# Local attention with queries transposed ahead of all scores; causal attention transposing 64-row halves in pairs; last attention mending its diagonal in 64-row halves

## The reference

```python
q = q * cos * scale + rotate_half(q) * sin * scale     # k likewise
sim = jnp.einsum('bhwie,bhwje->bhwij', bq, bk2) * QK_SCALE   # own window and the one before
attn = jax.nn.softmax(jnp.where(mask, -max, sim), -1)
out = jnp.einsum('bhwij,bhwje->bhwie', attn, bv2)
```

```python
sim = einsum('bhid,bhjd->bhij', q, k) - abs(i - j) * slope[h];  sim = where(causal, -max, sim)
out = einsum('bhij,bhjd->bhid', softmax(sim), v) @ w_out + b_out
```

```python
logits = einsum('bhqd,bhkd->bhqk', q, k) / SCALE - softplus(decay_alpha)[h] * abs(q - k)
out = einsum('bhqk,bhkd->bhqd', softmax(logits), v) @ out_w.T + out_b
```

## Time and profile before

| | |
|---|---|
| time, median of 3 runs | 4435.03 us (4434.4 to 4439.9) |
| profiled execution, its own time | 4430.25 us |
| span in its profile | 4428.5 us, mean granted TensorE clock 0.926 |
| busy | PE 3915.2 us (88%), DVE 3103.5 (70%), ACT 2556.6 (58%), POOL 1247.7 (28%) |

### The profile page before, as it was taken

How to read it: one execution, slowest core, us unless ns; L and a number is a source line. 1 busy time by engine, 2 the same in 40 slices (tenths; PEclk the granted TensorE clock), 3 DMA queues, 4 the chain that set the end, 5 groups by cost and what they waited for, 6 DMA issues and landing times.

```text
span 4428.5 us, 113349 instructions
## 1 busy us (share of the span) xinstructions
PE 3915.2 (88%) x46366; PEld 2158.4 (49%) x46462; DVE 3103.5 (70%) x5185; ACT 2556.6 (58%) x3768; POOL 1247.7 (28%) x1082
## 2 busy tenths in 40 slices
PE   3789999999999999867778999999997599999997
PEld 1365555555555555535553555555553233333333
DVE  7788888888888888645414666666664677777772
ACT  5456666666666667552224555555553276767774
POOL 0366656655566566310000000000000011111220
PEclk7899999999999999965578999999998699999998
DMA  0222222222222222201000000000000300000000
GB/s 18 71 67 75 69 65 80 71 72 74 65 76 72 68 76 68 55 10 24 21 9 17 3 4 4 4 2 4 4 1 26 100 19 20 19 20 19 19 2 15
DMA packets 85355, 166.74 MB, mean 38 GB/s; under 512 B 23336, under 2 KB 37336, under 8 KB 83568
## 3 DMA queue, kind: packets, MB, share of 16 engines
q1 hardware_dynamic: 84816, 159.13, 13.8%
HBM read 40.60 MB, written 8.52 MB: 11 GB/s over the span
## 4 chain that ended last, share of the span: by engine, by line
PE 46%; issue 19%; POOL 15%; DVE 12%; ACT 5%; DMA 1%; SPq 1%; POOLq 0%; DVEq 0%; ACTq 0%
POOL arena L987 7%; POOL arena L991 6%; PE banks L1287 6%; PE banks L2237 5%; PE banks L1270 4%; PE banks L1258 4%; ACT arena L2373 2%; PE banks L522 2%; PE banks L2195 2%; PE banks L2211 2%; PE banks L1306 1%; DVE arena L861 1%; DVE arena L1438 1%; PE banks L2215 1%; PE banks L605 1%
## 5 line engine op out<-in xcount | busy, mean ns | idle before, releaser
L2447 DVE TENSOR_REDUCE arena<-banks 128x2 f32<-128x1024 f32 x512 | 614.2, 1223 | 248.6 <-PE banks L2202 140.4
L2373 ACT ACTIVATE arena<-banks 128x1024 f32<-128x1024 f32 x512 | 522.8, 1025 | 252.7 <-PE banks L2218 134.2
L987 POOL TENSOR_TENSOR arena<-arena 128x512 f32<-128x512 f32 x384 | 424.5, 1127 | 637.4 <-DVE arena L870 629.8
L991 POOL TENSOR_TENSOR arena<-arena 128x1024 f32<-128x1024 f32 x192 | 533.1, 2776 | 15.1
L1438 DVE CUSTOM_DVE_ANT_0 arena<-arena,banks 128x512 f32<-128x512 f32 (+3 forms) x640 | 361.9, 603 | 202.6 <-issue 201.3
L1381 ACT ACTIVATE arena<-banks 128x512 f32<-128x512 f32 (+3 forms) x320 | 170.2, 532 | 401.7 <-PE banks L1270 401.0
L522 PE MATMUL banks<-arena 128*128 128x512 f32 x768 | 366.7, 622 | 30.8 <-issue 15.0
L2237 PE MATMUL banks<-arena 128*32 128x256 f32 x4096 | 334.4, 393 | 14.2 <-issue 8.7
L1518 POOL COPY arena<-arena 128x512 f32<-128x512 f32 x32 | 19.6, 613 | 1123.5 <-DVE arena L1464 1123.5
L1373 ACT ACTIVATE arena<-arena 128x128 f32<-128x128 f32 (+15 forms) x256 | 328.6, 1285 | 11.3 <-DVE arena L1450 6.3
L1258 PE MATMUL banks<-arena 64*128 64x512 f32 (+3 forms) x1280 | 322.3, 581 | 5.1 <-issue 3.8
(11 more groups left out here) (433 smaller groups left out, 7384.3 us busy)
## 6 DMA issues: line engine op xcount, KB each, us to landing
arena<-arena SPq DMA_DIRECT2D x768, 64.0 KB
arena<-arena SPq DMA_DIRECT2D x96, 384.0 KB, 3.6
arena<-arena SPq DMA_DIRECT2D x96, 128.0 KB, 3.4
arena<-in_lf_wqkv SPq DMA_DIRECT2D x6, 1024.0 KB, 6.0
arena<-features_k SPq DMA_DIRECT2D x32, 128.0 KB
arena<-arena SPq DMA_DIRECT2D x8, 512.0 KB
arena<-features_q SPq DMA_DIRECT2D x16, 216.0 KB
arena<-in_lf_wqkv SPq DMA_DIRECT2D x6, 512.0 KB, 3.8
```

The source lines that it names most:

```text
L987: nc.gpsimd.tensor_tensor(r[:, :, e * H2:(e + 1) * H2], q[:, j, :, (1 - e) * H2:(2 - e) * H2], s[:, j, 1, e * H2:(e + 1) * H2].unsqueeze(1 ...
L991: nc.gpsimd.tensor_tensor(a, a, lf_rb, ALU.add).then_inc(S("lf_rot" + x), 1)
L2373: nc.scalar.activation(bi_PT[n % 4], PS[:, 2 * bi_slot("S", n):2 * bi_slot("S", n) + 2].rearrange("p a b -> p (a b)"), ACT.Exp).then_inc(S ...
L2447: nc.vector.tensor_reduce(bi_max[j % 2][:, t, :, c], PS[:, 2 * slot:2 * slot + 2], AX.X, ALU.max).then_inc(S("bi_mx"), 1)
```

## The change

It has three parts.

1. Local attention: `scores` is one piece again instead of two halves, and `turn_q(s-1)` stands ahead of it, right behind `qk(s)`.
2. Causal attention: each 128 x 128 transpose becomes two, of the block's lower and upper 64 rows, 64 moving columns each. The lower halves of both heads go to bank 4, the upper ones to bank 5, and `at_PT` has one buffer for both heads. A turn starts only when both copies of the last one are done, and it signals both copies at its end. A `sem_inc` on TensorE carries the waits (one in each turn, two where b is 0). The copies have as many elements as before, in runs of 64.
3. Last attention: each mending is twelve matmuls of 64 rows, heads alternating, instead of six of 128; the two halves of the triangle are separate operands (`bi_trib` doubles, `bi_tri` triples to 384 KB and holds 64-row identities too), and the slopes are copied once for each half of the partitions (two short VectorE copies at the start).

```diff
@@ lf_pe, step
                 if lf_live(s, end):
                     qk(s, l)
-                if lf_live(s - 2, end):
-                    scores(s - 2, l, end, 0)
                 if lf_live(s - 1, end):
                     turn_q(s - 1, l, end)
                 if lf_live(s - 2, end):
-                    scores(s - 2, l, end, 1)
+                    scores(s - 2, l, end)
@@ at_pe, turn
+                n = min(4, at_row(c, x) + 1 - 4 * b)
+                if i >= 1:
+                    pe.wait_ge(S("at_ptA"), l * 80 + i)
+                    pe.wait_ge(S("at_ptB"), l * 80 + i)
                 for h in range(2):
                     if b == 0:
                         pe.wait_ge(S("at_exp"), l * 64 + (2 * (2 * c + x) + h + 1))
-                    if i >= 1:
-                        pe.wait_ge(S("at_ptB" if h else "at_ptA"), l * 80 + i)
-                    for j in range(min(4, at_row(c, x) + 1 - 4 * b)):
-                        m = nc.tensor.transpose(PS[:, 4 + h, j * P:(j + 1) * P], ck(at_E[c % 2][x][h], 4 * b + j, P), ident)
-                    m.then_inc(S("at_trB" if h else "at_trA"), 1)
+                        pe.sem_inc(S("at_turning"), 1)
+                    elif h == 0:
+                        pe.sem_inc(S("at_turning"), 1)
+                    for j in range(n):
+                        k = h * n + j
+                        lower = nc.tensor.transpose(PS[:, 4, k * at_D:(k + 1) * at_D], ck(at_E[c % 2][x][h], 4 * b + j, P)[0:at_D], ident[0:at_D, 0:at_D])
+                        upper = nc.tensor.transpose(PS[:, 5, k * at_D:(k + 1) * at_D], ck(at_E[c % 2][x][h], 4 * b + j, P)[at_D:P], ident[at_D:P, at_D:P])
+                lower.then_inc(S("at_trA"), 1)
+                upper.then_inc(S("at_trB"), 1)
@@ at_dve, turned (at_act's is the same for bank 5, columns at_D to P)
-                nc.vector.tensor_copy(at_PT[x][0][:, 4 * b:4 * b + n, t % 2 * P:(t % 2 + 1) * P],
-                                      PS[:, 4, 0:n * P].rearrange("p (a b) -> p a b", b=P)).then_inc(S("at_ptA"), 1)
+                nc.vector.tensor_copy(at_PT[x][:, :, 4 * b:4 * b + n, t % 2 * P:t % 2 * P + at_D],
+                                      PS[:, 4, 0:n * P].rearrange("p (h a b) -> p h a b", h=2, b=at_D)).then_inc(S("at_ptA"), 1)
@@ bi_pe, scores (logits likewise, with bi_trib's first half)
-                    for h in range(2):
-                        for x in range(3):
-                            m = nc.tensor.matmul(PS[:, 2 * slot + h, n:n + P], ck(bi_aI[p], 2 * x + h, P), bi_trib[:, P:2 * P], start=False, stop=x == 2)
+                    for y in range(6):
+                        for h in range(2):
+                            m = nc.tensor.matmul(PS[:, 2 * slot + h, n:n + P], ck(bi_aI[p], y, P)[rows(h)], ck(bi_trib, 2 + y % 2, P)[rows(h)], start=False, stop=y == 5)
```

More of the change, by code:

```diff
@@ L1166, in program @@
         at_E = [[[arena.f32(n) for _ in range(2)] for n in (T // 2, T)] for _ in range(2)]
-        at_PT = [[arena.f32_3(n, 2 * P) for _ in range(2)] for n in (NB // 2, NB)]
+        at_PT = [arena.f32(2 * n * 2 * P).rearrange("p (h k q) -> p h k q", h=2, k=n) for n in (NB // 2, NB)]
         at_mx = [arena.f32_3(2, 4) for _ in range(2)]
@@ L2033, in program @@
         bi_cut = arena.bf16(bi_H)
-        bi_slope = arena.f32_3(8, 8)
-        bi_a = [arena.f32(8) for _ in range(2)]
-        bi_tri = arena.f32(2 * P)
-        bi_trib = arena.bf16(2 * P)
+        bi_slope = arena.f32_3(8, 11)
+        bi_a = [arena.f32(11) for _ in range(2)]
+        bi_tri = arena.f32(6 * P)
+        bi_trib = arena.bf16(4 * P)
         bi_aI = [arena.bf16(6 * P) for _ in range(2)]
@@ L2492, in slopes @@
                 pool.wait_ge(S("bi_sa"), n + 1)
[L2493 to L2494 removed]
+                for y in range(6):
+                    m = nc.gpsimd.tensor_tensor(ck(bi_aI[p], y, P), ck(bi_tri, 4 + y % 2, P), bi_a[p][:, 8 + y // 2:9 + y // 2].broadcast_to([P, P]), ALU.mult)
                 m.then_inc(S("bi_ai"), 1)
```

51 lines of the change are left out of this document (26 added, 25 removed).

## The result

| | before | changed kernel |
|---|---|---|
| median | 4434.72 us (4 runs, 4429.8 to 4439.9) | 4356.83 us (4 runs, 4354.12 to 4366.32) |
| ratio to before | | 0.9828, 95% interval 0.9809 to 0.9847 |
| profiled execution, its span | 4428.5 us | 4352.3 us |

A forecast was written before the change was run, and what follows sets the result against it. TensorE was taken to bound causal and last attention, the order of waits the local one; 80 + 31 - 1.5 + 12 = 121.5 us off 4430.25 gave 4309, 4313 from the median, with 8 in 10 inside 4270 to 4378.

The forecast's parts named there:

- the first rival: Causal attention: a 64-row transpose's load takes 0.109 us, so only switches are saved there; 4373 us, chance 13%.
- The transposes' stream, 102 us: Causal attention: a pair of half transposes takes 0.062 us instead of 0.109 per block, over 2176 blocks, 102 us of TensorE.
- the slower rival: Causal transposes: the two halves' loads go one after the other, 0.109 each, a pair 0.218; 4609 us, chance 6%.
- the 129 us: Causal attention: TensorE time saved in all, by the transposes' stream and the net gain from switches.
- The causal switches, net 27: Causal attention: scores and turns share a shape, saving 37 and 12 us; 128-row work behind turns costs 22.
- What comes late next, 48 us: Causal attention: around short turns VectorE allows little of TensorE's saving; 1.5 us lost in each of 32 pairs of steps.
- The clock: Granted clock: the prediction read it as 2.4 GHz in causal and last attention and had no term for a fall.
- Increments, 0: Causal attention: TensorE's 448 `sem_inc`s taken as free; rival that they drain TensorE, 4398 us, chance 4%.
- The rival of the full gain: Causal and last attention: later long units absorb VectorE's lag and the held-back time comes too; 4274 us, chance 9%.
- the 11 us: Last attention, logits units: the part of 21 us saved there that is given back as waiting for VectorE.
- Last attention, 31 less 1.5: Last attention: mendings lose 42 us of switches, 21 + 10 counted; larger `bi_tri` and copies at the start cost 1.5.
- Local attention, 12 us: Local attention: switches between scores and transposes go, 0.21 us in 61 waits of L876, less 1 us for GpSimd's rotation.

The follow-up runs named there:

- e11_deep: Changed kernel with a turn's lower halves of both heads all before the upper ones, and mendings in alternating runs of three: 4403.62 us, ratio 0.9930.
- e8_late: Changed kernel with 192 more increments in causal turns, and local queries' transposes ahead of the mask only in three steps of four: 4352.71 us, ratio 0.9805.
- e1_a: Kernel before with only the local attention's part of the change: 4435.24 us, ratio 0.9996.
- e4_bc: Changed kernel with the local attention's part undone, so the causal and last attention's parts only: 4356.82 us, ratio 0.9818.
- e9: Changed kernel, causal attention: output projection ahead of the turn in an odd step's first unit, VectorE's normalisation ahead of logits: 4360.14 us, ratio 0.9835.
- e10: e9 plus, in an odd step's third unit, the first projection piece ahead of the turn and VectorE's L1481 ahead of logits: 4336.44 us, ratio 0.9777.
- e5_serial: Changed kernel with all lower, then all upper halves in each head's piece of a turn, and mendings six per head in a row: 4380.18 us, ratio 0.9869.
- e3_c: Kernel before with only the last attention's part of the change: 4398.25 us, ratio 0.9918.
- e12_act_copy_first: e10 plus ScalarE's copy of the turn ahead of its long exponential in a step's first two units: 4359.07 us, ratio 0.9823.
- e2_b: Kernel before with only the causal attention's part of the change: 4400.21 us, ratio 0.9922.
- e6_copy_first: Changed kernel with the local attention as before and VectorE's copy of a turn ahead of the next logits in all causal units: 4416.74 us, ratio 0.9952.
- e7_copy_first_some: Changed kernel with the local attention as before and VectorE's copy ahead of the logits in two causal units of ten: 4399.55 us, ratio 0.9915.

## Why the prediction was right, and where it was not

- **Direction, size, range**: faster, by 78 instead of 122 us, inside the range, outside the forecast's own range of 4285 to 4345. The causal attention missed by 40 us and the local one by its whole 12, against 11 us too little in the last. That the time is inside the range is in part luck: the part of the range above 4345 was there for the first rival (4373), whose mechanism is refuted, and another cost filled it.
- **The transposes' stream, 102 us**: right. The pair goes at 0.062 us, and the loads of one half follow each other at 0.06. My sign for the slower rival, halves over 0.03 us apart, was a bad one: 97 of 219 full turns show it and still keep the step of 0.062. The first rival, a load of 0.109, is refuted, and with it, for these loads, the rule of the Trainium skill ("TensorE: Matmul & The Clock Gate", "LDWEIGHTS (loading the stationary operand)") that it came from. The slower rival, halves one after the other, is refuted as well, but e11_deep shows that it lay near: with eight of a half in a row the causal part gives nothing. The stream is four fifths of the 129 us, not five sixths.
- **The causal switches, net 27**: some 15. By the distances between starts TensorE saves about 118 us, not 129. Scores to turn gains 0.09 and not 0.15 (the last score to the first transpose 0.52, now 0.43). Turn to 128-row work costs 0.09, not 0.15, but a projection piece of two matmuls now takes 1.06 us to the scores behind it instead of 0.95, and the output projection nearly as much more, 11 us in 114 places, which the sum has at nothing. Why is open.
- **What comes late next, 48 us**: the term that was sized too small. The place was right, the price was not: I let the stretch of the earlier trace rows shrink by 0.4 us, and it did not shrink at all (8.12 and 8.12); of its three likes one shrank by 0.25 us and two grew, by 0.08 and 0.68. I had looked for the limit in VectorE, 0.7 us of room, and between its copies 0.3 us did come. What took it back is what I had named last, ScalarE's long exponentials ahead of a copy that the next turn wants for both heads. I also had one wait per pair of steps, and the trace shows two to four, of 0.2 to 1.0 us. The waits came to about 69 us, from 118 less 40 less 9 for the clock; those that the profile names grew by 56.
- **The clock**: not in the prediction at all. In the changed kernel it fell in three places and at the branch's end, some 9 us, and in no kernel without the 64-row transposes.
- **Increments, 0**: right (e8_late).
- **The rival of the full gain** was added up wrong: the 48 and the 11 us are 59, not 40, so it stands for 4254 us and not 4274, outside the range that was to hold most of it.
- **Last attention, 31 less 1.5**: mechanism right, the give-back too high. The switches that go are worth 42 us, and 40.5 came: of the 11 us that I held back for VectorE in the logits units, 5 show as a longer wait of L2199, and the start cost nothing (first matmul to first exponential 91.0 us instead of 91.3). The round of four chunks went from 27.3 to 25.6 us, and most others by 1.1 to 1.2. The 1.5 us that are missing from the 42 are within the branch's scatter of 7.
- **Local attention, 12 us**: wrong. The scores do end 0.25 us earlier behind the projections, but L872 still waits for them as long as L876 did, and the values projection waits for ScalarE's copy instead (6.8 to 17.7 us):

```profile
DVE arena L872 <- PE banks L582: 41.3, 69, 4.8
```

  against 40.7 us and 61 times in the earlier trace rows, where I forecast 28. In steps where the reduction waits, it starts 0.41 us (median) after the last recorded score instead of 0.25, and so it does in e1_a (0.42), while e4_bc shows 0.25; this takes back most of what the earlier end gives. Where GpSimd's rotation is late the transposes wait 0.23 to 0.32 us, twice what I read. Why the reduction starts later after 128 scores in one run than after 64 stays open.

## What to carry to other kernels

Before an engine's saving is counted, follow for each stretch the rows of every engine that the next step waits for, and not the one with the highest busy share alone: here ScalarE, busy 6.08 of 8.12 us, ended the stretch, and VectorE with 7.70 did not. A change that makes a step wait for two engines instead of one can give back there what it gains (0.30 against 0.31 us). Where an engine gets faster between waits, its idle time grows, and its clock can fall with it: look at the granted clock behind each new wait. And when a wait for a copy is long, other work moved ahead of the waiting instruction can do more than moving the copy: here it gave 0 (e9) and 18 us more (e10), while moving the copy cost 43 to 60 us.

## What the hardware showed that I had not expected

- Matmuls of different row halves start out of program order, so TensorE does not begin its list strictly in order, as the opening has it. With four lower and four upper halves in turn in the program, the trace shows them starting in pairs at the full cadence of 0.062 us. In the full turns of e5_serial and e11_deep and the mending shown the first matmul of the second half starts ahead of three that stand before it, not more. With six in a row a mending takes 0.56 instead of 0.43 us to 128*32 work, with eight a full turn 0.89 instead of 0.58.
- The granted clock falls in the causal attention of every kernel that has the 64-row transposes, and in none without. Behind the first 60 us of the branch it is never at 1.2 GHz in before, e1_a and e3_c, and for 14 to 51 us in the eleven others: 14 in e10_make_first and e12_act_copy_first, 17 in e5_serial, 20 in e11_deep, 24 in e8_late and e9_out_first, 27 in the changed kernel, e2_b and e4_bc, 41 and 51 in e6_copy_first and e7_copy_first_some.
